# Cross attention in a fused Flamingo block: keys of four heads in one product, context product in three high/low passes, another order of the products

## The reference

```python
def _L1_xattn_ref(hidden_states, encoder_hidden_states, Wq, Wk, Wv, Wo, gq, gk):
    ...
    q = (hidden_states @ Wq).reshape(B, Sq, H, D)
    k = (encoder_hidden_states @ Wk).reshape(B, Skv, H, D)
    v = (encoder_hidden_states @ Wv).reshape(B, Skv, H, D)
    q = rmsnorm(q, gq)
    k = rmsnorm(k, gk)
    scores = jnp.einsum('bqhd,bkhd->bhqk', q, k) * scale
    attn = jax.nn.softmax(scores, axis=-1)
    out = jnp.einsum('bhqk,bkhd->bqhd', attn, v)
    out = out.reshape(B, Sq, H * D)
    return out @ Wo
```

## Time and profile before

| | before |
|---|---|
| median of 3 runs | 1146.96 us (1146.81 to 1147.1) |
| profiled execution, its own time | 1146.84 us |
| its span | 1145.0 us |
| TensorE busy | 989.2 us (86%) |
| VectorE busy | 743.0 us (65%) |
| ScalarE busy | 650.3 us (57%) |
| GpSimd busy | 515.6 us (45%) |
| mean granted TensorE clock | 0.935 of full speed |
| DMA in all | 35.94 MB |

### The profile page before, as it was taken

One profiled execution on the slowest core, in us unless ns is written; L12 is line 12 of the kernel. 1 busy time (PEld: TensorE's weight loads), 2 busy tenths in 40 slices (PEclk: granted clock), 3 DMA queues, 4 the chain that ended last, 5 costly groups with the idle time before them and its releaser, 6 DMA issues.

```text
span 1145.0 us, 15771 instructions
## 1 busy us (share of the span) xinstructions
PE 989.2 (86%) x5567; PEld 800.0 (70%) x5567; DVE 743.0 (65%) x1297; ACT 650.3 (57%) x1269; POOL 515.6 (45%) x512
## 2 busy tenths in 40 slices
PE   5276766669999998999878999888989999899898
PEld 1032222348999997999767888777878888778787
DVE  6899998865555556555436565676665766577575
ACT  5857634746666676677533666624657544443443
POOL 0366541025666665566523444443443544354352
PEclk7599878879999999999989999999999999899999
DMA  9101000044000000000050000000000400000000
GB/s 317 78 1 55 0 1 0 1 151 179 1 1 1 1 1 1 2 1 1 1 201 1 1 1 1 1 1 1 1 1 1 182 25 1 1 1 1 19 1 19
DMA packets 4692, 35.94 MB, mean 31 GB/s; under 512 B 1022, under 2 KB 2150, under 8 KB 3110
## 3 DMA queue, kind: packets, MB, share of 16 engines
q1 hardware_dynamic: 4613, 34.93, 7.9%
HBM read 33.88 MB, written 1.05 MB: 31 GB/s over the span
## 4 chain that ended last, share of the span: by engine, by line
PE 54%; DVE 17%; ACT 7%; issue 6%; ACTq 0%; DVEq 0%; POOL 0%; POOLq 0%
PE psum L378 13%; PE psum L380 13%; PE psum L379 13%; PE psum L618 4%; DVE f_h_lo L1577 4%; PE psum L606 2%; ACT f_silu L1069 2%; PE psum L560 2%; DVE f_silu L1560 2%; DVE x_norm L1111 2%; PE psum L564 1%; DVE f_silu L1569 1%; PE psum L682 1%; PE psum L717 1%; ACT a_P L985 1%
## 5 line engine op out<-in xcount | busy, mean ns | idle before, releaser
L378 PE MATMUL psum<-x_norm_T_hi,f_wgu_hi 128*128 128x512 f32 x400 | 177.7, 444 | 0.0
L1569 DVE TENSOR_TENSOR f_silu<-f_silu,psum 128x512 f32<-128x512 f32 x100 | 68.8, 688 | 165.8 <-ACT f_silu L1069 165.8
L764 ACT ACTIVATE f_h_hi<-f_silu 128x512 fp32r<-128x512 f32 x100 | 63.0, 630 | 173.2 <-DVE f_silu L1560 172.7
L380 PE MATMUL psum<-x_norm_T_hi,f_wgu_lo 128*128 128x512 f32 x400 | 161.2, 403 | 0.0
L379 PE MATMUL psum<-x_norm_T_lo,f_wgu_hi 128*128 128x512 f32 x400 | 160.6, 402 | 0.0
L378 PE MATMUL psum<-f_wd_hi,f_h_hi 128*128 128x256 f32 x400 | 121.7, 304 | 13.2 <-DVE f_h_lo L1577 13.2
L1577 DVE TENSOR_TENSOR f_h_lo<-f_silu,f_h_hi 128x512 fp32r<-128x512 f32 x100 | 123.7, 1237 | 3.6 <-ACT f_h_hi L764 3.5
L1646 POOL TENSOR_TENSOR f_wgu_lo<-f_wa,f_wgu_hi 128x512 fp32r<-128x512 f32 x44 | 56.6, 1287 | 144.7 <-ACT f_wgu_hi L764 144.6
L379 PE MATMUL psum<-f_wd_lo,f_h_hi 128*128 128x256 f32 x400 | 114.2, 286 | 0.0
L380 PE MATMUL psum<-f_wd_hi,f_h_lo 128*128 128x256 f32 x400 | 113.9, 285 | 0.0
L1718 POOL TENSOR_TENSOR m_dBu<-m_du,m_Bs 128x1024 f32<-128x1024 f32 x32 | 76.1, 2380 | 76.7 <-DVE m_du L1206 24.8
(11 more groups left out here) (289 smaller groups left out, 2695.2 us busy)
## 6 DMA issues: line engine op xcount, KB each, us to landing
f_wa<-in_f1a SPq DMA_DIRECT2D x1, 8448.0 KB, 24.9
f_w<-in_f3w SPq DMA_DIRECT2D x1, 5376.0 KB, 15.5
w_raw<-in_w0raw SPq DMA_DIRECT2D x1, 3072.0 KB, 18.4
f_w<-in_f2w SPq DMA_DIRECT2D x1, 3072.0 KB, 14.5
f_wb<-in_f1b SPq DMA_DIRECT2D x1, 2304.0 KB, 8.2
a_wo<-in_wo SPq DMA_DIRECT2D x2, 1024.0 KB, 13.1
a_wq<-in_wq SPq DMA_DIRECT2D x1, 2048.0 KB, 26.6
x_res<-in_x SPq DMA_DIRECT2D x1, 1024.0 KB, 9.5
```

Source lines behind the costliest of these rows:

```text
L378: mm(out, wh, xh, start=start, stop=False, **kw)
L380: return mm(out, wl, xh, start=False, stop=stop, **kw)
L764: return A(out_, in_, ACT.Copy)
L1569: V.tensor_tensor(sg[g % 2][:, :], sg[g % 2][:, :], ps[:, 3 + 2 * (g % 2), :], ALU.mult).then_inc(S("f_m"), 1)
```

## The change

- **Keys of four heads.** The key weights of all heads are split into high and low parts once, in F0 (`a_wk_hi` on ScalarE and `a_wk_lo` on GpSimd, 128x2048 each), and a product takes one token tile and four heads: `mm3` of 512 columns (`keys`). Step 0 makes four such units (all four token tiles of heads 0 to 3), each of steps 1 to 28 makes one unit of a later group, and steps 29 to 31 make none. Squares and scaled keys go to `a_k_tok`, two buffers of four tiles by four heads. The per-head weight parts (`parts`) then hold the query weights only. At step 0 squares, sums and scaling are of 2048 columns, and the power is of 16 columns in place of 4.
- **Context product.** `ctx_tok` is split (`a_ctx_tok_hi` on ScalarE, `ctx_tok_lo` on GpSimd, 128x1024 each, once, at the start of A1). ScalarE's copy of the transposed probabilities now gives the high part (`a_PT_hi`), and a new subtraction on VectorE (`probs_lo`, 128x1024, in each step) the low part. The product is `mm3`, 12 matmuls of 256 columns.
- **Order.** TensorE's step i becomes: queries of i+1, one key unit, context product of i-2, scores of i, query sums of i+1, transposes of i-1, key transposes of i+1, output product of i-2. The residual, statistics and normalisation of the first half come one step later on VectorE, ahead of the reciprocal instead of behind it.
- `a_ctxT`'s split moves from tile 6 to tile 4 of F0. `f1a` holds 10 tiles and `f1b` 18, because the new buffers need room.

The diff, cut to what the text speaks of:

```diff
@@ -34,7 +34,7 @@
     GU, WJ = 2 * KC * P, 2 * KC * P + DM
-    J1A = 22
+    J1A = 10
     MAGIC = 1.5 * 2.0 ** 23
...
@@ -527,61 +536,72 @@
             loaded(pe, "wq", "wk", "ctk")
-            pe.wait_ge(S("q_h"), 2 * NT)
-            pe.wait_ge(S("xT_ready"), 1)
             pe.wait_ge(S("a_ctx"), 1)
+            pe.wait_ge(S("a_wk"), 1)
+            def keys(i):
+                units = range(TH) if i == 0 else (i + TH - 1,)
+                for n in units:
+                    g, t = n // TH, n % TH
+                    sl = slice((g // 4) * HALF + t * P, (g // 4) * HALF + (t + 1) * P)
+                    wsl = slice((g % 4) * HALF, (g % 4 + 1) * HALF)
+                    if i == 0 and t == 2:
+                        pe.wait_ge(S("xT_ready"), 1)
+                    last = mm3(ps[:, (4, 5, 2, 3)[t] if i == 0 else 7, :], ch[:, sl], cl[:, sl], wkh[:, wsl], wkl[:, wsl], True, True)
+                last.then_inc(S("a_k"), 1)
...
                 xh, xl = (xTh, xTl) if i < HEADS else xTa
+                if i == 0:
+                    keys(0)
+                    pe.wait_ge(S("q_h"), 2 * NT)
                 pe.wait_ge(S("a_w"), i + 1)
-                if i:
-                    pe.wait_ge(S("a_kT"), i)
                 if i == HEADS:
                     pe.wait_ge(S("xT_ready"), 2)
-                for t in range(TH):
-                    sl = slice((i // HEADS) * HALF + t * P, (i // HEADS) * HALF + (t + 1) * P)
-                    ksl = slice(t * P, (t + 1) * P)
-                    last = mm3(ps[:, 7, ksl], ch[:, sl], cl[:, sl], hi[:, KC * P:AQ], lo[:, KC * P:AQ], True, True)
-                last.then_inc(S("a_k"), 1)
                 if i:
...
                 last.then_inc(S("a_q"), 1)
-            def norm_transpose(i):
+                if 0 < i < KB:
+                    pe.wait_ge(S("a_kT"), i)
+                    keys(i)
+            def query_sums(i):
...
                 last.then_inc(S("a_qn"), 1)
-                pe.wait_ge(S("a_ktok"), i + 1)
+            def keys_T(i):
+                pe.wait_ge(S("a_ktok"), min(i + 1, KB))
+                if i >= KB:
+                    pe.wait_ge(S("a_kT"), i)
                 for t in range(TH):
-                    last = nc.tensor.transpose(ps[:, 7, t * P:(t + 1) * P], ktok[:, t * P:(t + 1) * P], ident[:, :])
+                    last = nc.tensor.transpose(ps[:, 7, t * P:(t + 1) * P], ktok[i // 4 % 2][:, t, i % 4, :], ident[:, :])
                 last.then_inc(S("a_kt"), 1)
...
             keys_queries(0)
-            norm_transpose(0)
+            query_sums(0)
+            keys_T(0)
+            pe.wait_ge(S("a_ctk"), 1)
             for i in range(HEADS2 + 2):
...
                     keys_queries(i + 1)
-                if i == 2:
-                    pe.wait_ge(S("xT_ready"), 2)
                 if i >= 2:
-                    pe.wait_ge(S("a_al"), i - 1)
-                    pe.wait_ge(S("a_vol"), i - 1)
-                    if i == HEADS + 2:
-                        pe.wait_ge(S("a_res"), 1)
-                    for t in range(TH):
-                        sl = slice(t * P, (t + 1) * P)
-                        last = mm3(ps[:, t // 2, (t % 2) * DM:(t % 2 + 1) * DM], ah[:, sl], al[:, sl],
-                                   voh[i % 2][:, :], vol[i % 2][:, :],
-                                   (i - 2) % HEADS == 0 and t % 2 == 0, (i - 2) % HEADS == HEADS - 1, skip_group_check=True)
-                    last.then_inc(S("a_out"), 1)
+                    pe.wait_ge(S("a_ptl"), i - 1)
+                    for b in range(2):
+                        for kv in range(2):
+                            last = mm3(ps[:, 4, b * DM:(b + 1) * DM], *(c[:, ((i - 2) // HEADS) * TH + 2 * b + kv, :] for c in (ctkh, ctkl)),
+                                       *(p[:, b, kv * DM:(kv + 1) * DM] for p in (PTh, PTl)), kv == 0, kv == 1)
+                    last.then_inc(S("a_ac"), 1)
                 if i == 0:
...
@@ -596,6 +616,8 @@
                     last.then_inc(S("a_s"), 1)
+                if i + 1 < HEADS2:
+                    query_sums(i + 1)
                 if 1 <= i <= HEADS2:
...
@@ -610,14 +632,20 @@
                 if i + 1 < HEADS2:
-                    norm_transpose(i + 1)
-                if 1 <= i <= HEADS2:
-                    pe.wait_ge(S("a_pts"), i)
-                    for b in range(2):
-                        for kv in range(2):
-                            last = mm(ps[:, 4, b * DM:(b + 1) * DM], ctk[:, ((i - 1) // HEADS) * TH + 2 * b + kv, :],
-                                      PT[:, b, kv * DM:(kv + 1) * DM], start=kv == 0, stop=kv == 1)
-                    last.then_inc(S("a_ac"), 1)
+                    keys_T(i + 1)
+                if i == 2:
+                    pe.wait_ge(S("xT_ready"), 2)
+                if i >= 2:
+                    pe.wait_ge(S("a_al"), i - 1)
+                    pe.wait_ge(S("a_vol"), i - 1)
+                    if i == HEADS + 2:
+                        pe.wait_ge(S("a_res"), 1)
+                    for t in range(TH):
+                        sl = slice(t * P, (t + 1) * P)
+                        last = mm3(ps[:, t // 2, (t % 2) * DM:(t % 2 + 1) * DM], ah[:, sl], al[:, sl],
+                                   voh[i % 2][:, :], vol[i % 2][:, :],
+                                   (i - 2) % HEADS == 0 and t % 2 == 0, (i - 2) % HEADS == HEADS - 1, skip_group_check=True)
+                    last.then_inc(S("a_out"), 1)
             pe.wait_ge(S("a_out"), HEADS2)
...
@@ -905,9 +932,11 @@
                     quantised_inputs(1)
-                if t == NT - 2:
+                if t == SPLIT_AT:
                     copy(ch[:, :], ctxT[:, :]).then_inc(S("a_ch"), 1)
                     loaded(act, "wq", "wk")
+                    copy(wkh[:, :], wk[:, :]).then_inc(S("a_wkh"), 1)
+                if t == NT - 2:
                     parts(0)
...
@@ -932,12 +961,20 @@
-                act.wait_ge(S("a_k"), i + 1)
+                if i < KB:
+                    act.wait_ge(S("a_k"), i + 1)
+                if i == 0:
+                    for b in range(2):
+                        last = A(Pm[b][:, :, :], ps[:, 4 - 2 * b:6 - 2 * b, :], ACT.Square)
+                    last.then_inc(S("a_ksq"), 1)
+                elif i < KB:
+                    g, t = (i + TH - 1) // TH, (i + TH - 1) % TH
+                    if g >= 2:
+                        act.wait_ge(S("a_kt"), 4 * (g - 1))
+                    A(ktok[g % 2][:, t, :, :].rearrange("p n d -> p (n d)"), ps[:, 7, :], ACT.Square).then_inc(S("a_ksq"), 1)
+                act.wait_ge(S("a_q"), i + 1)
                 if i:
                     act.wait_ge(S("a_qn"), i)
-                A(ksq[:, :], ps[:, 7, :], ACT.Square).then_inc(S("a_ksq"), 1)
-                act.wait_ge(S("a_q"), i + 1)
-                act.wait_ge(S("a_rks"), i + 1)
                 A(qsq[:, :], ps[:, 6, :], ACT.Square).then_inc(S("a_qsq"), 1)
...
@@ -954,14 +991,16 @@
+            act.wait_ge(S("q_hq"), NT)
+            copy(ctkh[:, :, :], ctk[:, :, :]).then_inc(S("a_ctkh"), 1)
             norm_T(1, (2, 3), xTh)
...
             for i in range(HEADS2 + 1):
+                if i + 1 < HEADS2:
+                    squares(i + 1)
                 if i >= 2:
                     ac_hi(i - 2)
-                if i + 1 < HEADS2:
-                    squares(i + 1)
                 if i + 2 < HEADS2:
...
@@ -972,7 +1011,7 @@
                         act.wait_ge(S("a_ac"), i - 1)
-                    copy(PT[:, :, :], ps[:, 4:6, :]).then_inc(S("a_pts"), 1)
+                    copy(PTh[:, :, :], ps[:, 4:6, :]).then_inc(S("a_pts"), 1)
                 if i + 1 < HEADS2:
...
@@ -1387,6 +1438,11 @@
                 V.tensor_tensor(al[:, :], ps[:, 4, :], ah[:, :].bitcast(f32), ALU.subtract).then_inc(S("a_al"), 1)
+            def probs_lo(i):
+                dve.wait_ge(S("a_pts"), i + 1)
+                V.tensor_tensor(PTl[:, :, :], ps[:, 4:6, :], PTh[:, :, :].bitcast(f32), ALU.subtract).then_inc(S("a_ptl"), 1)
...
@@ -1395,11 +1451,13 @@
             for i in range(HEADS2):
+                if i + 1 < KB:
+                    key_norms(i + 1)
+                if i + 1 < HEADS2:
+                    queries_lo(i + 1)
                 if i >= 2:
                     ac_lo(i - 2)
-                if i + 1 < HEADS2:
-                    key_norms(i + 1)
-                    queries_lo(i + 1)
+                if i + 1 < KB:
                     keys_scaled(i + 1)
...
@@ -1413,19 +1471,25 @@
                     keys_lo(i + 1)
+                if i:
+                    if i > 1:
+                        dve.wait_ge(S("a_ac"), i - 1)
+                    probs_lo(i - 1)
+                if i == HEADS + 2:
+                    dve.wait_ge(S("a_out"), HEADS)
+                    residual("A1", 0)
+                    V.tensor_copy(scratch[:, 12:13], epsc[:, :]).then_inc(S("a_res"), 1)
+                if i == HEADS + 3:
+                    stats(0)
+                if i == HEADS + 4:
```

(24 more changed lines are left out.)

58 lines of the change are left out of this document (40 added, 18 removed).

## The result

| | before | changed |
|---|---|---|
| median of 4 runs | 1147.0 us (1146.81 to 1147.1) | 1126.89 us (1125.73 to 1129.23) |
| ratio, with 95% interval | | 0.9828 [0.9814, 0.9842] |
| profiled execution, its own time | 1146.84 us | 1126.31 us |
| its span | 1145.0 us | 1123.8 us |
| TensorE, VectorE, ScalarE, GpSimd busy | 989.2, 743.0, 650.3, 515.6 us | 952.9, 777.7, 643.4, 505.8 us |

The changed kernel is faster by 20.1 us in the medians and by 20.5 us in the profiled executions; 1125.3 was forecast, with a range of 1119 to 1138, and both the median and the profiled execution lie in it.

What follows compares the result with a forecast made beforehand. TensorE, busy throughout settled steps of A1, was taken as the bound. From 1146.84 us: steps -31.3 and -1.2, change of halves +0.9, F0 +1.4, start of A1 +7.8, end +0.9, total -21.5, giving 1125.3 us; range 1119 to 1138.

Steps and rivals of the forecast that it cites:

- Settled step: Step of A1 bound by TensorE: from 9.66 to 8.58 us, by wider keys, split context product and a wait gone.
- The subtraction: New VectorE pass in each A1 step, ahead of the context product: 1.22 us, its wait covered by barely 0.1.
- The walk through it: Loop in an A1 step from score transposes through copy and subtraction to the context product: 8.54 us.
- Rival B: Loops in A1 bind earlier: a step of 9.1, 14.5 us of the gain lost, about 1139 us; chance 0.20.
- D: Subtraction in A1 runs at GpSimd's pace, 2.36 us: a step of 9.7, 1157.8 us, slower; chance 0.04.
- E: Subtraction pass near 1.9 us: the step gains 0.4, the start takes it back, no change; chance 0.02.
- Start: Added work in F0 (+1.4 us) and the longer chain at the start of A1 before the first scores (+7.8).
- Change of halves: Excess over settled steps where A1 changes halves: 5.9 us before, 6.8 after, so +0.9.
- The residual wait: In step 18 TensorE's output product waits for the residual behind the subtraction: 4.7 us lost once.
- Statistics and normalisation: At the change of halves, now ahead of the reciprocal: about 2 us more in the two steps after.
- The end of A1: Last probabilities pass copy, subtraction and product in turn: +1.2 us for the subtraction, -0.35 for the product, +0.9.
- Rival C: In F0 GpSimd's key-weight subtraction holds up VectorE's clamp: 2.5 us join the path, 1127.8 us; chance 0.11.

Runs made afterwards that it cites:

- e5: Changed kernel with each key unit issued as four pieces of 128 columns instead of one of 512; 1150.93 us, ratio 1.0022.
- e3: Changed kernel with the context product in plain fp32 again, without the subtraction or the split of the context tokens; 1127.4 us, ratio 0.9826.
- e4: Changed kernel with a second, unused VectorE pass of the same size ahead of the new subtraction in each step; 1165.23 us, ratio 1.0148.
- e1: Changed kernel with the first half's residual moved from step 18 to step 17, behind the reciprocal; 1123.55 us, ratio 0.9787.
- e2: Changed kernel with GpSimd's low part of the context tokens ahead of its powers instead of behind them; 1125.85 us, ratio 0.9809.
- e8: Changed kernel with the edits of e1, e2 and e6 together; 1117.97 us, ratio 0.9745.
- e6: Changed kernel with GpSimd's subtraction of the key weights in F0 cut into four instructions of 512 columns; 1126.57 us, ratio 0.9825.

## Why the prediction was right, point by point

- **Settled step, 8.58 forecast, 8.53 measured.** The keys' unit was put at 0.70 and takes 0.74; the context product was put at 1.45 and takes 1.51; output product and queries take 2.71 and not 2.84, and that closes the sum. e5 gives 0.65 for the width of the keys (0.63 forecast) and e3 gives 0.30 for the three passes (0.35).
- **The subtraction, 1.22 forecast.** It takes 1.21. The walk through it gave 8.54 and through GpSimd 8.45; steps without a key unit take 8.45, and e4 shows 0.07 of room. Rival B, loops that bind earlier, is out, and D and E, which wanted a pass of 1.9 us or more, with it.
- **Start, +1.4 in F0 and +7.8 in A1.** The first scores moved from 259.85 to 269.05, 9.2 in all, the very sum, but the parts were off and that is luck. ScalarE's copy of the transposed input moved by 3.13, of which the copy of `ctx_tok` ahead of it is 0.95 (1.0 forecast) and F0 2.2, where I had 1.4. From there to the first scores it is 6.07 more, where I had 6.8. F0 was under-priced by more than that: the normalisation in it moved by 3.4 (237.08 to 240.50), with the held clamp in the way, and this one execution got 1.2 back as its next group of matmuls ran at the full clock; in e1, e2, e4 and e5 F0 costs 3.1 to 3.5 by the same measure. In A1 the power of 16 columns took 1.88 more than that of 4, where I had 1.5, and the three groups of TensorE before the scores, priced at 5.7 at half the clock, took 5.02. The first `a_max` moved by 9.99: it now starts 2.55 behind the first scores and not 1.76, and those 0.8 I did not have. The copy of the transposed input, before and then after:

```profile
242.99 1.08 ACT L764 ACTIVATE x_norm_T_hi<-psum 128x512 fp32r<-128x512 f32 x2
```

```profile
246.12 1.08 ACT L792 ACTIVATE x_norm_T_hi<-psum 128x512 fp32r<-128x512 f32 x2
```

- **Change of halves, 6.8 forecast, 10.1 measured.** This is the term that was most wrong. The residual wait was right (4.7 forecast, 4.6 measured). "Statistics and normalisation cost about 2 more in the two steps after" was not: I priced them on VectorE alone and left out that GpSimd's power of 1.01 then stands ahead of the keys' power. With the residual out of the way (e1) 5.2 were left, of which the comparison with e8 puts 2.65 on the clock behind the gap. I had no term for the clock there.
- **Why the sum was right all the same.** The steps gave 30.8 where the terms make 31.6 (31.3 + 1.2 - 0.9). The 3.3 missed at the change of halves were for the most part made up by the last four steps, which without a key unit are 7.39, 8.46, 8.45 and 8.45 where I had counted all 29 alike at 8.58 (1.6), and by 0.05 in each of the other 25 (1.2). That makes 2.8, and 0.3 more is spread over the rest. The end of A1 was put at +0.9 and took 0.91 more. The -1.3 behind A1, for which I had no term, went against the +0.8 at the first `a_max` and is no more than such executions differ by. So the mechanism of the settled step was right and its size too; that the whole came out within 1 us is in part luck, as misses of 3.3 and 2.8, of 0.8 and 0.7, and of 0.8 and 1.3 cancelled.
- **Rival C**, given 0.11, came true as a mechanism: the clamp took 3.26. Its price was put at 2.5; with 2.0 of the hold removed (e6) F0 is 1.8 shorter at the normalisation and 1.5 to 1.8 at the copy of the input. The forecast left it out, and the 1.4 for F0 was too low for that reason.
- **`f1b`**, costed at nothing behind 20 us of transfer: it landed in 19.3, and no engine's waits behind A1 name it.

```profile
f_wb<-in_f1b SPq DMA_DIRECT2D x1, 6912.0 KB, 19.3
```

## What to carry to other kernels

Where TensorE is full, issuing the same columns in wide matmuls instead of narrow ones is worth doing; here 1536 columns went from 1.45 to 0.74 us, and without that the change gained nothing. A batch four times as large at the start of a loop, and one-off work ahead of an instruction that other engines wait for, take part of it back, and they can be moved: put a one-off pass into the idle time of its own engine, cut to fit it, and hand a large batch on in halves. Price a moved one-off on every engine that it passes through, and count what TensorE may lose at half its clock behind a gap as well as the gap. Before a part of a difference is laid to an edit, look whether it lies behind the place of the edit, and whether more than one execution shows it: a single profile of the changed kernel made e6 look like a gain that was lost.

## What the runs showed of the hardware that I had not expected

- GpSimd's power is priced by the column: 1.01 us for 4 columns of 128, 1.63 for 8, 2.89 for 16, so about 0.16 a column beyond a fixed 0.4.
- A VectorE pass that GpSimd blocks is held by one GpSimd instruction, not by its whole work: 3.26 beside one of 4.52 (six kernels), 1.24 to 1.26 beside four that make 5.41 (five kernels). Cutting GpSimd's work in four cost GpSimd 0.9.
- A gap of 1.67 us on TensorE was followed by the lower clock in e1 (granted 0.50 over the next 4 us) and by none in e8, with the same instructions around it. At a later gap of 1.74 us it was the other way round. The first is worth 2.65 us, and single comparisons of a microsecond or two between such kernels can't be read without the clock's row.
